# Masked cross-attention turned in strips of 64 rows, and another order of two queues within an expert's tile

## What is computed

```python
# first stage, for each of 128 sequences
scores = jnp.einsum('bhqd,bhkd->bhqk', q, k) / np.sqrt(D_K)
scores = jnp.where(mask[:, None, :, :] > 0, NEG, scores)
p = jax.nn.softmax(scores, axis=-1)
x = jnp.einsum('bhqk,bhkd->bhqd', p, v)
...
# last stage, for each of 8 experts
h = jax.nn.gelu(t @ w1[e] + b1[e])          # 256 -> 1024
y = h @ w2[e] + b2[e]                       # 1024 -> 256
out = jnp.where((routes == e)[:, None], y, out)
```

## Time and profile before

| what | us |
|---|---|
| median of 3 runs (lowest, highest) | 2874.72 (2873.59, 2875.07) |
| the profiled execution's own time | 2873.39 |
| its span, first to last instruction | 2871.6 |
| granted TensorE clock over the span | 0.933 of full speed |
| busy over the span | PE 85%, DVE 75%, ACT 68%, POOL 55% |

### The profile page before, as it was taken

The page is one execution under the profiler, slowest core; times in us unless marked ns, Lnnn a source line. Parts: engine busy times, 40 slices in busy tenths (PEclk is TensorE's granted clock), DMA queues, the critical chain, the costliest instruction groups (busy, mean ns, idle before and its releaser), DMA issues. The chain is left out here.

```text
span 2871.6 us, 96041 instructions
## 1 busy us (share of the span) xinstructions
PE 2442.8 (85%) x37734; PEld 1929.7 (67%) x37734; DVE 2156.5 (75%) x4991; ACT 1948.5 (68%) x4323; POOL 1579.3 (55%) x1680
## 2 busy tenths in 40 slices
PE   3999999999946999994969999999957887508997
PEld 2788888888834777762548888888846666506665
DVE  4899999999965999984447677777757887645665
ACT  2788888888847999962437777777736665335554
POOL 3777777777723555531027666766626776053444
PEclk9999999999976999997979999999978999559999
DMA  5222222222100000000022122212100000641110
GB/s 156 63 73 73 71 70 70 70 70 70 48 16 1 1 1 1 1 1 31 1 70 69 55 66 69 69 54 68 52 18 2 2 2 2 222 162 42 42 39 27
DMA packets 120676, 145.06 MB, mean 51 GB/s; under 512 B 12912, under 2 KB 111632, under 8 KB 118064
## 3 DMA queue, kind: packets, MB, share of 16 engines
q1 hardware_dynamic: 115568, 124.40, 14.5%
q0 software_dynamic: 4672, 14.57, 1.4%
HBM read 123.71 MB, written 15.22 MB: 48 GB/s over the span
## 5 line engine op out<-in xcount | busy, mean ns | idle before, releaser
L2068 DVE TENSOR_TENSOR_SCAN m_s<-m_a,m_psBx 128x2048 f32<-128x2048 f32 x64 | 282.7, 4417 | 21.6 <-PE m_psBx L1843 18.8
L1364 DVE SCALAR_TENSOR_TENSOR x_pTl<-x_psS,x_pTh 128x1024 f16<-128x1024 f32 x128 | 156.7, 1225 | 173.8 <-ACT x_pTh L1272 173.8
L662 ACT ACTIVATE x_prob<-x_prob,x_low 128x257 f32<-128x257 f32 x512 | 253.5, 503 | 9.8 <-DVE x_low L789 9.6
L1854 PE MATMUL m_psS<-m_s,all_ident 128*128 128x256 f32 x1024 | 238.4, 386 | 0.9 <-DVE m_s L2068 0.9
L1854 PEld LDWEIGHTS m_psS<-m_s,all_ident 128*128 128x128 f32 x1024 | 190.7, 191 | 43.3 <-issue 18.2
L789 DVE CUSTOM_DVE_ANT_0 x_prob<-x_psS,x_masked,x_prob 128x256 f32<-128x256 f32 x512 | 216.0, 477 | 1.1 <-PE x_psS L546 0.9
L1975 ACT ACTIVATE m_a<-m_dt,m_rate 128x248 f32<-128x248 f32 x512 | 205.8, 489 | 5.0 <-DVE m_s L2068 4.6
L678 ACT ACTIVATE x_kh<-x_psK,x_bk 128x256 f16<-128x256 f32 x256 | 107.5, 470 | 118.1 <-PE x_psK L430 118.1
L3015 POOL TENSOR_TENSOR e1t_hidl<-e1t_g,e1t_hidh 128x512 f16<-128x512 f32 x78 | 92.8, 1189 | 144.3 <-ACT e1t_hidh L2987 144.3
L804 DVE SCALAR_TENSOR_TENSOR x_pTl<-x_psT,x_pTh 128x512 f16<-128x512 f32 x256 | 163.2, 677 | 0.9 <-PE x_psO L572 0.9
L1053 POOL TENSOR_TENSOR x_qbdh<-x_qh,all_mask4h 128x1024 f16<-128x1024 f16 x32 | 60.6, 1895 | 181.1 <-DVE x_ql L1345 181.1
(11 more groups left out here) (554 smaller groups left out, 10247.5 us busy)
## 6 DMA issues: line engine op xcount, KB each, us to landing
x_ctx<-in_ctxT SPq DMA_DIRECT2D x64, 1024.0 KB, 6.2
x_mraw<-in_mask SPq DMA_DIRECT2D x128, 128.5 KB, 2.8
e1r_stage<-in_L_ffn_w SPq DMA_DIRECT2D x16, 1024.0 KB, 5.1
e_rows<-e1r_pad POOLq DMA_DIRECT2D x1, 5070.0 KB, 19.5
e1t_row<-e_rows SPq DMA_DIRECT2D x39, 130.0 KB, 2.1
all_xres<-in_x SPq DMA_DIRECT2D x1, 4096.0 KB, 14.5
x_vxr<-x_vx SPq DMA_DIRECT2D x128, 32.0 KB, 3.6
x_vxr<-x_vx SPq DMA_DIRECT2D x96, 8.0 KB, 2.3
```

Of the source, the lines that this page charges most:

```text
L662: act.activation(prob[c % 4][:, h, :], prob[c % 4][:, h, :], ACT.Exp, bias=low[c % 4][:, h:h + 1], scale=-1.0, accum_out=sm[c % 2][:, h:h ...
L1364: dve.scalar_tensor_tensor(pT[c % 4][1][:].rearrange("p r k n -> p (r k n)"), psS[c % 2][:], PS, pT[c % 4][0][:].rearrange("p r k n -> p ( ...
L1854: last = pe.matmul(psS[:, h * ST:(h + 1) * ST], con["ident"][:], S[h][:, :, m, :], start=m == 0, stop=m == NS - 1)
L2068: dve.tensor_tensor_scan(rows(S), rows(A), psBx[:], 0.0, ALU.mult, ALU.add).then_inc(scan_done, 1)
```

## The change

In the first stage each 128x128 transpose becomes two of 64 rows: the same 128 columns of `prob` as the stationary operand, but the rows of one half only, and 64 columns of the identity as the moving one. The two strips `r` go to the two banks of `psT`, so the copies on ScalarE and VectorE go over strips in place of context halves, with the same number of columns (512) and a destination in runs of 64. In the last stage the queues of ScalarE and VectorE get another order within a tile.

```diff
+        def turned(t, r):
+            return t[:].rearrange("p k (h r s) -> p r k h s", r=RG, s=64)[:, r]
+
+        def strip_of(t, r):
+            return t[:, r * 512:(r + 1) * 512].rearrange("p (k h s) -> p k h s", k=2, h=4)
...
                 for kt in range(2):
                     for h in range(4):
-                        last = pe.transpose(psT[:, kt * 512 + h * P:kt * 512 + (h + 1) * P],
-                                            prob[c % 4][:, h, kt * P:(kt + 1) * P], con["ident"][:])
+                        for r in range(RG):
+                            rows, to = slice(64 * r, 64 * r + 64), r * 512 + (kt * 4 + h) * 64
+                            last = pe.transpose(psT[:, to:to + 64], prob[c % 4][rows, h, kt * P:(kt + 1) * P],
+                                                con["ident"][rows, rows])
...
-                for kt in range(2):
-                    act.activation(pT[c % 2][0][:, kt, :], psT[:, kt * 512:(kt + 1) * 512], ACT.Copy, scale=PS)\
-                        .then_inc(pt_hi, 1)
+                for r in range(RG):
+                    act.activation(turned(pT[c % 2][0], r), strip_of(psT, r), ACT.Copy, scale=PS).then_inc(pt_hi, 1)
...
-                    dve.scalar_tensor_tensor(pT[c % 2][1][:, kt, :], psT[:, kt * 512:(kt + 1) * 512], PS,
-                                             pT[c % 2][0][:, kt, :], ALU.mult, ALU.subtract).then_inc(pt_lo, 1)
+                    dve.scalar_tensor_tensor(turned(pT[c % 2][1], r), strip_of(psT, r), PS,
+                                             turned(pT[c % 2][0], r), ALU.mult, ALU.subtract).then_inc(pt_lo, 1)
...
                     if exists(i, c, 0):
-                        take_low(i, c, 0)
                         if exists(i, c, 1):
                             hi_xn(*at(i, c, 1))
+                        take_low(i, c, 0)
+                        take_low(i, c, 1)
                         gelu(i, c, 0)
                         hi_hid(i, c, 0)
-                        take_low(i, c, 1)
                         gelu(i, c, 1)
                         hi_hid(i, c, 1)
...
-                    if exists(i, c, 2):
-                        normalise(*at(i, c, 2))
                     if exists(i, c, 1):
                         lo_xn(*at(i, c, 1))
                     if exists(i, c, 0):
                         add_bias(i, c, 0)
                         add_bias(i, c, 1)
+                    if exists(i, c, 2):
+                        normalise(*at(i, c, 2))
                     if exists(i, c, -1):
                         finish(*at(i, c, -1))
```

More of the change, by code:

```diff
@@ L799, in lo_pT @@
                 b = i * 8 + c
-                for kt in range(2):
-                    dve.wait_ge(pt_hi, b * 2 + (kt + 1))
-                    if kt == 0:
+                for r in range(RG):
+                    dve.wait_ge(pt_hi, b * 2 + (r + 1))
+                    if r == 0:
                         wait(dve, pv_mm, b - 1)
-                    dve.scalar_tensor_tensor(pT[c % 2][1][:, kt, :], psT[:, kt * 512:(kt + 1) * 512], PS,
-                                             pT[c % 2][0][:, kt, :], ALU.mult, ALU.subtract).then_inc(pt_lo, 1)
+                    dve.scalar_tensor_tensor(turned(pT[c % 2][1], r), strip_of(psT, r), PS,
+                                             turned(pT[c % 2][0], r), ALU.mult, ALU.subtract).then_inc(pt_lo, 1)
             def lo_px(i, c):
```

## The result

The changed kernel takes 2881.26 us (median of 9 runs, 2880.23 to 2887.01) against 2875.56 (9 runs, 2873.59 to 2878.49) of the kernel before on the same chip: ratio 1.0023, with 95% confidence between 1.0012 and 1.0033, so 0.2% slower, little but clear of none. Forecast were 2845 us, in a range of 2830 to 2872. The profiled execution took 2880.23 us, its span is 2878.4; before it was 2871.6, so 6.8 us came on.

What follows compares the result with a forecast made beforehand. Nearly full TensorE and VectorE, linked in a ring, were taken to bound cross-attention, and VectorE and ScalarE waiting in turn the experts' tiles. 2873.4 - 12 (strips) - 18 (tiles) = 2843.4, plus 1.3 for the median: 2845 us, range 2830 to 2872.

Steps and rivals of the forecast that it cites:

- The strips give 0.19 us a step: Cross-attention: a step's transposes on TensorE fall from 0.87 to 0.68 us, in each of 128 steps.
- the pair: Two strip transposes, one of each strip, running at once on TensorE: 0.055 us a pair, eight pairs a step.
- The entry: On TensorE, from the last keys' matmul to the first strip transpose of a step: 0.249 us.
- The prediction's step from 96 to 128 columns: TensorE loads of 125 and 141 ns, 0.5 ns a column, taken as half of what the skill's rule gives.
- the 190 ns of L1854 are a double load: The true f32 product's load on TensorE, read as a double load of 190 ns, supporting about 0.06 us for 128 columns.
- Two of four steps of a group count, 12 us: Cross-attention: two of a group's four transpose blocks lie in the ring, 0.38 us a group, 12 us over 31 groups.
- Runs of 64 cost nothing: Copies on ScalarE and VectorE into destinations in runs of 64 take no longer; costed at nothing.
- The wait for GpSimd's low half goes: Experts' tiles: TensorE's idle time before `outputs`, 0.50 us a tile, disappears, 18.6 us over 37 tiles.
- TensorE sets the tile at 6.27: Experts' tiles: with VectorE and ScalarE well under it, TensorE's 6.77 - 0.50 = 6.27 us becomes the tile.
- The narrowest place: Experts' tiles: the moved normalisation ends 2.2 us after `hidden`, its transpose is due at 2.6; 0.4 us to spare.
- The tile gains nothing: Rival, experts' tiles: something outside the rows keeps TensorE at 6.77 us a tile, total 2863 us; chance 0.07.

Runs made afterwards that it cites:

- e4_dve_alone: The kernel before with only VectorE's new order in the experts' tiles (normalise behind both sums), ScalarE's order and transposes as before: 2953.77 us, ratio 1.0265.
- e3: The kernel before with both new orders of the experts' tiles (VectorE's and ScalarE's), without the strips: 2892.91 us, ratio 1.0053.
- e5: The kernel before with only ScalarE's new order in the experts' tiles (both copies ahead of gelu and split): 2852.19 us, ratio 0.9928.
- e11: e9_norm_second with the experts' numbers loaded into registers without declared bounds: 2997.61 us, ratio 1.0422.
- e10: The changed kernel with VectorE's old order put back, and the load of the next tile's expert issued twice on TensorE: 2867.12 us, ratio 0.9967.
- e9_norm_second: The changed kernel with VectorE's normalisation between the low half of the next input and the first sums: 2839.85 us, ratio 0.9883.
- e8: The changed kernel with its sixteen strip transposes reordered, all eight of one strip and then the other's eight: 2904.21 us, ratio 1.0097.

## Why the prediction was wrong, step by step

- *The strips give 0.19 us a step.* They give 0.133. The mis-sized term is the pair: 0.063 and not 0.055, and 0.112 for the first. The entry was cheaper than forecast. The rule of the Trainium skill ("TensorE: Matmul & The Clock Gate", section on LDWEIGHTS) that a load takes its columns over 1.2 in ns would have 107 ns between loads; these f32 loads pass every 63 in a single strip, and those of different strips side by side, so here it does not hold as a price, while its rule that loads of different row groups overlap does. The prediction's step from 96 to 128 columns, 16 ns, is 0.6 of what the same rule gives for 32 columns, 27 by estimate, and not half, and that the 190 ns of L1854 are a double load no run shows; neither moves the sum.
- *Two of four steps of a group count, 12 us.* The stage gained 11.2, but as 2.6 steps of 0.133 and not as 2 of 0.19. A right sum from two errors.
- *Runs of 64 cost nothing.* 2 ns. Right.
- *The wait for GpSimd's low half goes.* Right. *TensorE sets the tile at 6.27.* The size is right with ScalarE's order alone (6.27), the reason wrong: its queue, not its array.
- *The narrowest place: the normalisation ends 2.2 us after `hidden`, and its transpose is due after `outputs`, at 2.6, so 0.4 to spare.* This is the step that failed. It ended 2.12 us after `hidden` (2704.55 - 2702.43; forecast 2.2), and for the array 0.5 was to spare. But the queue comes to that wait 0.97 us after the end of `hidden` (2703.40), loses 1.15 there, and the 0.75 us of load and address behind it can't be hidden any more. I computed when the matmul was due and not when the instruction was due in its queue. In place of 18 us gained stand 19.6 lost.
- *The tile gains nothing, "such as the transpose at the narrow place"*, was among the rivals, with a chance of 0.07 and 6.77 as its floor. I let the tile fall back to what it was, and had no reason for that floor: a new ring has a length of its own, 7.33.

The whole error is 2881.3 - 2845 = 36 us, and the tiles alone make 19.6 + 18 = 37.6.

## What to carry to other kernels

An instruction of TensorE that waited held up everything behind it in the queue (1.15 us in a tile of the changed kernel, 2.7 in e4_dve_alone), also work that the array's rows don't show: register loads, addresses, assertions. Where operands are addressed by registers, price each such operation (0.124 us here), ask when the queue and not the array comes to a wait, and put work that waits for nothing ahead of work that does. And price a moved step by the ring that it closes, not by the slack of the tile as it was: the same move on VectorE cost 78 us with ScalarE's old order (e4 against the kernel before) and 39 with its new one (e3, 17.0 above the kernel before on its chip, against e5, 21.9 below it on its own).

## What the runs showed of the hardware that was not expected

- TensorE's sequencer set the pace of `hidden`, whose matmuls are addressed by a register, once a head start was used up: one register operation of 46 ns every 0.124 us, one every 0.201 us with an assertion of 18 ns ahead of it (e11). In `outputs` one operation served two matmuls and still came every 0.124 us, so the price is the operation's and not the matmul's. The load of a register took 0.30 us, with what follows it 0.63 in all (the second one of e10).
- Declaring a register's bounds once costs one assertion a load; without them one came at each use, and some 155 us with it (e11 against e9_norm_second, each against the kernel before on its chip).
- A strip of 64 rows takes 128 f32 columns of stationary operand every 63 ns, though each such load shows 138 ns.
- The strips' transposes overlap between strips even when they aren't alternated, in e8 after the first five had started.
- The profile's busy share of TensorE rose from 231 to 247 of 250 us while 7% fewer matmuls were done in the time.
